# A causal attention stage on Trainium2: score tiles made once and kept, values as the moving side

## The reference

```python
x = layernorm(x + linear_attention(x))      # stage A, 16 heads, chunks of 64
x = layernorm(x + fp8_gated_ffn(x))         # stage B, hidden 2048
x = layernorm(x + causal_attention(x))      # stage C, one head of width 128
x = layernorm(x + base + low_rank_experts(x))  # stage D, 6 experts of rank 16, top 2
```

```python
q, k, v = x @ Wq + bq, x @ Wk + bk, x @ Wv + bv
scores = q @ k.T / sqrt(128)                # causal mask: -inf above the diagonal
out = softmax(scores) @ v @ Wo + bo
```

## Time and profile before

| | |
|---|---|
| time, three runs | 1518.12, 1520.05, 1521.35 us; median 1520.05 |
| the profiled execution's own time | 1522.29 us |
| its span, first to last instruction | 1520.5 us |
| granted TensorE clock, mean of the span | 0.989 |
| TensorE matmul busy | 1463.3 us, 96% |
| TensorE weight loads busy | 1004.2 us, 66% |
| VectorE busy | 1008.0 us, 66% |
| ScalarE busy | 734.4 us, 48% |
| GpSimd busy | 344.0 us, 23% |

### The profile page before, as it was taken

How to read it: one execution, slowest core, us unless ns; L and a number is a source line. 1 busy time by engine, 2 the same in 40 slices (tenths; PEclk the granted TensorE clock), 3 DMA queues, 4 the chain that set the end, 5 groups by cost and what they waited for, 6 DMA issues and landing times.

```text
span 1520.5 us, 23833 instructions
## 1 busy us (share of the span) xinstructions
PE 1463.3 (96%) x9472; PEld 1004.2 (66%) x9472; DVE 1008.0 (66%) x1966; ACT 734.4 (48%) x1039; POOL 344.0 (23%) x259
## 2 busy tenths in 40 slices
PE   8999999999999999899999999989999999999998
PEld 6677777777777776444554555546656666677886
DVE  3355555464646467888778778874888888566665
ACT  4333333333333335777877876853434444432333
POOL 0021211120211123000000000001657676750001
PEclk9999999999999999999999999999999999999999
DMA  7203031212130251001100100013100000000112
GB/s 269 81 27 109 28 110 33 104 55 89 49 108 1 87 188 42 14 1 56 56 28 28 56 29 27 1 42 114 37 1 1 1 0 1 0 1 28 56 56 83
DMA packets 43905, 79.93 MB, mean 53 GB/s; under 512 B 7074, under 2 KB 14882, under 8 KB 42387
## 3 DMA queue, kind: packets, MB, share of 16 engines
q1 hardware_dynamic: 43794, 78.41, 15.3%
HBM read 53.24 MB, written 25.17 MB: 52 GB/s over the span
## 4 chain that ended last, share of the span: by engine, by line
PE 63%; issue 19%; DVE 13%; ACT 3%; POOL 1%; DMA 0%; SPq 0%; DVEq 0%; POOLq 0%; ACTq 0%
PE psum L125 13%; PE psum L127 12%; PE psum L126 12%; PE psum L1360 6%; PE psum L1003 3%; PE psum L1010 3%; PE psum L616 2%; DVE sm L464 2%; PE psum L1338 2%; PE psum L642 2%; PE psum L631 2%; PE psum L637 2%; DVE c_mx L1281 1%; PE psum L651 1%; PE psum L646 1%
## 5 line engine op out<-in xcount | busy, mean ns | idle before, releaser
L1003 PE MATMUL psum<-early,high 128*128 128x512 fp8e4 x1024 | 235.0, 382 | 7.9 <-DVE low_r L975 4.2
L1003 PEld LDWEIGHTS psum<-early,high 128*128 128x128 fp8e4 x1024 | 98.2, 98 | 127.7 <-ACT early L880 6.6
L1209 POOL TENSOR_TENSOR c_ls<-c_ls,c_pr 128x512 f32<-128x512 f32 (+2 forms) x136 | 161.9, 1190 | 65.5 <-ACT c_pr L1254 56.3
L410 POOL TENSOR_TENSOR rms<-ms,mhalf 128x16 f32<-128x16 f32 x30 | 87.8, 2926 | 341.9 <-DVE ms L473 341.9
L1254 ACT ACTIVATE c_pr<-c_sc 128x512 f32<-128x512 f32 (+2 forms) x144 | 85.1, 593 | 152.7 <-DVE c_sc L1296 137.7
L1360 PE MATMUL psum<-c_pr,V 128*128 128x512 f32 (+2 forms) x288 | 138.1, 565 | 3.7 <-ACT c_pr L1254 2.5
L125 PE MATMUL psum<-Qh_r,Kh 128*128 128x512 f32 (+1 forms) x272 | 139.7, 513 | 0.0
L1010 PE MATMUL psum<-high,b_act 128*128 128x512 fp8e4 x512 | 118.9, 387 | 2.4 <-DVE Ql_r L980 2.2
L1296 DVE TENSOR_TENSOR c_sc<-psum,c_mb 128x512 f32<-128x512 f32 (+2 forms) x144 | 91.8, 640 | 42.8 <-PE psum L127 32.7
L125 PE MATMUL psum<-early_r,high_r 128*128 128x512 f32 x256 | 106.6, 417 | 5.4 <-DVE early_r L436 5.4
L127 PE MATMUL psum<-Qh_r,Kl 128*128 128x512 f32 (+1 forms) x272 | 105.2, 387 | 0.0
(11 more groups left out here) (238 smaller groups left out, 3245.8 us busy)
## 6 DMA issues: line engine op xcount, KB each, us to landing
low<-x_dram SPq DMA_DIRECT2D x9, 1024.0 KB, 5.5
wst<-in_L_ffn_w_gating SPq DMA_DIRECT2D x16, 512.0 KB, 4.5
xs<-in_L_attn_x SPq DMA_DIRECT2D x8, 1024.0 KB, 7.3
xt<-in_x_turned SPq DMA_DIRECT2D x7, 1024.0 KB, 5.0
x_dram<-xs SPq DMA_DIRECT2D x7, 1024.0 KB, 4.8
x_dram<-low SPq DMA_DIRECT2D x5, 1024.0 KB, 4.3
wst<-in_L_ffn_w_linear SPq DMA_DIRECT2D x16, 256.0 KB, 4.5
high<-x_dram SPq DMA_DIRECT2D x4, 1024.0 KB, 6.6
```

The costliest lines, as they stand in the source:

```text
L410: nc.gpsimd.tensor_tensor(rms_of(b, c), ms_of(b, c), const["mhalf"][:, 0:H], ALU.pow).then_inc(*done)
L1003: last = t.matmul(out[:, h, :], w8g[:, tile + k, (2 * m + h) * P:(2 * m + h + 1) * P], x8[:, u, k, :], start=k == 0, stop=k == DC - 1)
L1209: nc.gpsimd.tensor_tensor(ls[:, i % 2, q0:], ls[:, i % 2, q0:], pr[:, g % SLOTS, q0:], ALU.add).then_inc(*L.done(*name))
```

## The change

The scores of a tile are made once (`r`, three matmuls and the mask, keys as rows). ScalarE, for every fourth tile VectorE, copies them to a place on chip; VectorE takes the maximum with a running tile `gm` of 128 x 512, element by element. When a whole block is there, `gT` transposes `gm` (4 transposes), one reduction gives `nm` for all four chunks, and `dm`, `mb` follow as before. Then GpSimd adds `mb` in place, two tiles at a time (five pairs of the last block on VectorE), ScalarE takes the exponential in place over both, and `pv` multiplies: the exponentials are now the stationary side, 128 queries by 128 keys, and the values with a column of ones, 129 wide, the moving side. The ones give the row sums, so `ls`, `sum` and `L` go. The totals of all blocks after the first lie in banks 5 and 6; `on` copies them, `oT` transposes them (4 transposes), and `oh`, `ol`, `y` follow as before.

The places (`homes`) are pairs of tiles: 5 of their own, 6 in `Qh` and `Ql` where the queries are no longer wanted, and 8 in `xs` of blocks 0 to 3, which are stored to DRAM after their `norm` and loaded again for stage D (`spill`). Stage D therefore takes the blocks in the order 4, 5, 6, 0, 1, 2, 3, 7, and its weights are split into `Qh` and `Ql` when their last tiles are used. `order` says when scores are made by a table (`points`) of how many should be there at how many used, if a home is open. Stage C's first jobs now stand among stage B's last ones.

The diff, cut to its core:

```diff
+    homes = [("rows", n) for n in range(OWN)] + [(w, b) for b in (0, 2, 4) for w in ("Qh", "Ql")] + [("x3", n) for n in range(2 * SPILL)]
...
+    def home_of(home):
+        w, n = home
+        if w == "rows":
+            return rows[:, 2 * n - 2:2 * n, :] if n else first_rows[:, :, :]
+        if w == "x3":
+            return high[:, n // 2, 2 * (n % 2):2 * (n % 2) + 2, :]
+        return (Qh32 if w == "Qh" else Ql32)[:, n:n + 2, :]
...
+    raws = [("r", i, k) for i in range(NB) for k in range(tiles(i))]
+    points = [(4, 16), (9, 24)] + [(2 * (i + 1) * (i + 2) - 8, 2 * (i + 2) * (i + 3)) for i in range(2, NB - 1)] + [(10 ** 6, len(raws))]
...
+    def open_home():
+        for home in sorted(unused, key=lambda h: (h[0] not in ("Qh", "Ql"), last_use.get(h, (0, 0))[0])):
+            w, n = home
+            _, i, k = raws[made]
+            if i >= NB - 2 and k >= 2 * NB and w in ("Qh", "Ql"):
+                continue
+            if home in last_use or w == "rows" or (w == "x3" and n // 2 in ended and sum(x[0] == "pv" for x in order[ended[n // 2]:]) >= 6) or (w in ("Qh", "Ql") and made >= 2 * (n + 2) * (n + 3)):
+                return home
+        return None
+    def emit_raw():
+        nonlocal made
...
+    def emit_pv(i, k, n):
+        order.append(("pv", i, k))
+        if k % 2 or n == 2:
+            home = place[i, k // 2]
+            unused.append(home)
+            last_use[home] = (len(order), ("pv", i, k))
...
+    emit_raws(4)
+    order += [("gT", 0), ("bias", 0), ("mb", 0)]
+    for k in range(CH):
+        if k % 2 == 0:
+            emit_raws(2)
+        emit_pv(0, k, 1)
+    emit_raws(6)
+    order.append(("gT", 1))
+    emit_raws(2)
+    order.append(("mb", 1))
+    consumed, since = CH, 0
+    for i in range(1, NB):
+        outputs = [("oT", i - 1)] + [("y", i - 1, c) for c in range(CH)]
+        for u, (k, n) in enumerate(units(i)):
+            while made < len(raws) and made < wanted(consumed + n) and emit_raw():
+                pass
+            whole_block = i + 1 < NB and made >= 2 * (i + 2) * (i + 3)
+            if whole_block and since >= 2 and ("gT", i + 1) not in order:
+                order.append(("gT", i + 1))
+                since = 0
+            elif whole_block and since >= 2 and ("mb", i + 1) not in order:
                 order.append(("mb", i + 1))
-            order.append(("pv", i, k))
-            if tail and (k == 1 or k >= 3):
-                order.append(tail.pop(0))
-        order += tail
-    order += [("L", NB - 1)] + [("y", NB - 1, c) for c in range(CH)]
+            emit_pv(i, k, n)
+            consumed += n
+            since = since + n if whole_block else 0
+            if outputs and (u != 1 or i == 1):
+                order.append(outputs.pop(0))
+                if not outputs:
+                    ended[i - 1] = len(order)
+        order += outputs
...
+        if i + 1 < NB:
+            while made < 2 * (i + 2) * (i + 3):
+                assert emit_raw()
+            order += [x for x in (("gT", i + 1), ("mb", i + 1)) if x not in order]
+            since = 0
+    order += [("oT", NB - 1)] + [("y", NB - 1, c) for c in range(CH)]
+    on_dve = {x[1:] for n, x in enumerate(raws) if n % 4 == 3}
...
+    subs_on_dve = {(NB - 1, k) for k in range(2, CH * (NB - 1), 6)}
+    def soften(i, k):
+        while to_sub and to_sub[0] <= (i, k + 9):
+            x = to_sub.pop(0)
+            (dve_order if x in subs_on_dve else pool_order).append(("sub", *x))
+        while to_exp and to_exp[0] <= (i, k + 5):
+            act_order.append(("exp", *to_exp.pop(0)))
...
+        if kind == "r":
+            (dve_order if name[1:] in on_dve else act_order).append(("cp", *name[1:]))
+            dve_order.append(("max", *name[1:]))
+            if name[1:] == (1, CH):
+                pool_order.append(("bo", NB - 1))
+        elif kind == "gT":
+            dve_order.append(("nm", i))
+            act_order += [("dm", i, q) for q in range(CH)]
+            if i:
+                pool_order.append(("bo", i - 1))
...
+        elif kind == "mb":
+            act_order.append(("mb", i))
+            to_sub += [(i, k) for k, _ in units(i)]
+            to_exp += [(i, k) for k, _ in units(i)]
+            soften(i, -3)
+        elif kind == "pv":
+            soften(i, name[2])
+            if name[2] == tiles(i) - 1:
+                act_order.append(("on", i))
+                dve_order.append(("rl", i))
+        elif kind == "oT":
...
+            w, n_r = (4, 5)[n_r % 2] if n_r < 4 else n_r % (2 if i < 2 else 3), n_r + 1
...
+        banks[name] = (w,) if kind != "pv" else (5, 6) if i else (2, 3)
...
+    def totals(i):
+        w = 5 if i else 2
+        return psum[:, w:w + 2, 0:2 * VN].rearrange("p b (u n) -> p b u n", u=2)
...
+    def spill(sp):
+        for b in range(SPILL):
+            wait_for(sp, 0, (A, ("norm", b, CH - 1)))
+            sp.dma_start(x3_dram[b], xs[b]).then_inc(spilled[b], 16)
+        for b in range(SPILL):
+            sp.wait_ge(spilled[b], 16)
+            for half in range(2):
+                if ("x3", 2 * b + half) in last_use:
+                    wait_for(sp, 0, (M, last_use["x3", 2 * b + half][1]))
+            sp.dma_start(xs[b], x3_dram[b]).then_inc(back_in[b], 16)
...
+                wait_for(pool, 0, (A, ("mb", i)), copied(i, k), copied(i, k + (k < CH * i)))
+                if k < CH * i:
+                    both = home_of(place[i, k // 2])
+                    nc.gpsimd.tensor_tensor(both, both, mb[i % 2][:, None, :].broadcast_to([P, 2, BT]), ALU.add).then_inc(*L.done(*name))
                 else:
-                    wait_for(pool, 0, (L, ("sum", i, k - 1)))
-                    nc.gpsimd.tensor_tensor(ls[:, i % 2, q0:], ls[:, i % 2, q0:], pr[:, g % SLOTS, q0:], ALU.add).then_inc(*L.done(*name))
+                    q0 = (k - CH * i) * P
+                    row = row_of(i, k)[:, q0:]
+                    nc.gpsimd.tensor_tensor(row, row, mb[i % 2][:, q0:], ALU.add).then_inc(*L.done(*name))
...
+            if kind == "cp":
+                k = name[2]
+                q0 = max(0, k - CH * i) * P
+                copy_needs(act, i, k)
+                nc.scalar.activation(row_of(i, k)[:, q0:], bank_of("r", i, k)[:, q0:], ACT.Identity).then_inc(*A.done(*name))
+            elif kind == "on":
+                wait_for(act, 0, (M, ("pv", i, tiles(i) - 1)), *([(M, ("oT", i - 1))] if i else []))
+                nc.scalar.activation(on[:, :, :].rearrange("p (b u) n -> p b u n", u=2), totals(i)[:, :, :, 0:P], ACT.Identity).then_inc(*A.done(*name))
...
+            else:
+                k = name[2]
+                wait_for(act, 0, less_max(i, k))
+                if k < CH * i:
+                    both = home_of(place[i, k // 2])
+                    nc.scalar.activation(both, both, ACT.Exp, scale=scale).then_inc(*A.done(*name))
+                else:
+                    row = row_of(i, k)[:, (k - CH * i) * P:]
+                    nc.scalar.activation(row, row, ACT.Exp, scale=scale).then_inc(*A.done(*name))
...
+            elif kind == "max":
+                k = name[2]
...
+                if (i, k) not in on_dve:
+                    needs.append((A, ("cp", i, k)))
+                wait_for(dve, 0, *needs)
+                if k == 0:
+                    nc.vector.tensor_copy(out, row).then_inc(*done)
+                else:
+                    nc.vector.tensor_tensor(out, row, out, ALU.max).then_inc(*done)
...
-                nc.vector.reciprocal(rl[:, :], bank_of("L", i)[:, 0:CH]).then_inc(*done)
+                wait_for(dve, 0, (M, ("pv", i, tiles(i) - 1)), (A, ("on", i)), *([(V, ("y", i - 1, CH - 1))] if i else []))
+                nc.vector.reciprocal(rl[:, :].rearrange("p (b u) -> p b u", u=2), totals(i)[:, :, :, P]).then_inc(*done)
...
+            elif kind == "r":
...
+            elif kind == "gT":
+                wait_for(pe, 0, *needs, (V, ("max", i, tiles(i) - 1)))
+                for c in range(CH):
+                    last = nc.tensor.transpose(out[:, c * P:(c + 1) * P], gm[:, i % 2, c * P:(c + 1) * P], ident[:, :])
+            elif kind == "mb":
+                wait_for(pe, 0, *needs, (A, ("dm", i, CH - 1)))
+                last = nc.tensor.matmul(out[:, :], oner, dm, start=True, stop=True, skip_group_check=True)
             elif kind == "pv":
                 k = name[2]
-                g = sum(tiles(j) for j in range(i)) + k
-                q0 = max(0, k - CH * i) * P
-                keys = slice(k * P, (k + 1) * P)
+                n = 2 if k < CH * i else 1
                 wait_for(pe, 0, *needs, (A, ("exp", i, k)))
-                last = nc.tensor.matmul(out[:, q0:], values[:, keys], pr[:, g % SLOTS, q0:], start=k == 0, stop=k == tiles(i) - 1, skip_group_check=True)
-            elif kind == "L":
-                wait_for(pe, 0, *needs, (L, ("sum", i, tiles(i) - 1)))
+                for tile in range(k, k + n):
+                    row = row_of(i, tile)
```

(33 more changed lines are left out.)

305 lines of the change are left out of this document (150 added, 155 removed).

## The result

The changed kernel took 1557.19 us (median of four runs, 1555.43 to 1558.38) against 1520.11 us before: ratio 1.024, 95% interval 1.0223 to 1.0257. It is slower by 37 us, and I had forecast 18 us faster.

A forecast was written before the change was run, and what follows sets the result against it. Stage C was taken to be bound by TensorE with a tenth of slack. Work -28.2, pauses +(41 - 29), stage B's filled gaps -2 gave -18 us from a median of 1520.05: 1502 us, range 1493 to 1512.

The forecast's parts named there:

- What TensorE saves: TensorE's work in stage C: maxima, `L` and old values products removed, new values products and transposes added, -28.2 us.
- rival (c): New values products: weight loads don't hide beneath matmuls, 1056 x 0.11 us more, 1615 us; chance 0.03.
- the sum of the pauses: Stage C: TensorE's pauses, 41 us against 29 before; under 30 or over 55 would show the prediction wrong.
- The copy `on` and `rl` that free banks 5 and 6 (0.9 us) lie inside these.: Block boundaries: freeing the totals' banks adds nothing to the exposed pauses, which sum to 26.3 us.
- queued behind exponentials that wait for GpSimd: Block starts: ScalarE's copies wait, and TensorE waits for the banks, 0.5 to 1 us a block, 4 in all.
- The serial chain: Block boundaries: `gT` to `mb` 3.0 us and `mb` to first `pv` 4.7, partly covered; 26.3 us exposed in all.
- Stage D's roundings: Block 7: weight roundings moved there, 5 x 0.6 us on ScalarE and 5 x 0.69 on VectorE, cost nothing.
- if stage B or D changes by more than 5: Stages B and D: a change of more than 5 us in either would show the prediction wrong.
- The clock: Block boundaries: granted clock falls to 0.50 after pauses, at most one counted per boundary, 4 x 1.8 = 7 us.
- (a): Block boundaries cost little and the clock holds: pauses 15 to 25 us, 1476 to 1486 us; chance 0.24.
- (b): GpSimd's pair additions set the pace if over 3.2 us each; at 4.0 the time is 1543 us; chance 0.10.
- (d): VectorE takes over in units with a `y`, needing 4.5 us; gain cancelled, no change, 1520 us; chance 0.05.

The follow-up runs named there:

- run 1: The changed kernel with the totals' copy `on` ahead of the next block's first exponentials in ScalarE's order: 1541.14 us.
- run 5: The changed kernel with `on` ahead of the next block's first exponentials and exponentials queued 3 tiles ahead of their product instead of 5: 1537.77 us.
- run 12: The last kernel of Runs 9 to 11 with all eight score copies of block 1 on VectorE, which did two before: 1516.04 us.
- run 7: Run 5's kernel with `nb` as a product on GpSimd, and the last block's five pair additions also on GpSimd instead of VectorE: 1532.28 us.
- Runs 9 to 11: Added in turn to run 7: `bo` behind its block's last addition, 1526.19 us; `nm` ahead of queued statistics, 1525.06; blocks 1 to 7's first pair tile by tile, 1519.24.
- after: The changed kernel as first made, against the kernel before at 1520.11 us: 1557.19 us, ratio 1.024.
- runs 6 and 7: The first is run 5's kernel with `nb` as a product on GpSimd and means negated on VectorE: 1533.62 us; the second is run 7.
- run 4: The changed kernel with extra unread products in blocks 1 to 7, eight between `gT` and `mb`, ten ahead of the first `pv`: 1560.99 us.
- Run 3: The changed kernel without the addition of the negated maxima, the exponential's scale a hundredth as large; part of the computation is left out: 1509.7 us.
- run 13: Run 12's kernel with stage D's five weight roundings on VectorE behind the rounded parts of its first four x tiles: 1513.93 us.
- run 8: Run 5's kernel with the first pair addition of blocks 1 to 7 on VectorE instead of GpSimd: 1543.95 us.

## Why the prediction was wrong

**What TensorE saves: right.** Forecast -28.2 us, measured about -26. The passes step by 0.111 us with their weight loads beneath (rival (c) falls). The pair addition (2.4) and the pair exponential (1.05) cost what they were priced at. The rule of the Trainium skill that I had weighed there (page "TensorE: Matmul & The Clock Gate", Part 3, "The mechanism": a load overlaps matmuls in flight only in another row group) would make the step 0.22 us, by the forecast's estimate; the trace does not agree, with 0.111. A sentence earlier in the same section also lets a load run ahead that goes to a background weight buffer; the trace does not speak against that one.

**The failed step** is the sum of the pauses, forecast as 41 us against 29 before. In the account above, over a wider stretch, pauses and rest are 110 us against 48: 62 us more where I had 12. By the forecast's own measure, the 336.8 us from first to last `pv` less the 242 of work that its sums leave are some 95 us, far over the 55 that it had named as a sign of being wrong. The first part of the step is the sentence "The copy `on` and `rl` that free banks 5 and 6 (0.9 us) lie inside these." They don't lie inside; they stand behind. I priced the copy's own length and not its place in ScalarE's in-order queue, behind two exponentials that are each held by a 2.35 us addition, themselves behind a `bo` of 4.57, and at block 4 behind two normalizations too. The three boundaries where `rl` ends the pause took 17.8 us, and were priced at 9.6; moving `on` alone gave back 16 us (run 1). The second part is the sentence on ScalarE's copies "queued behind exponentials that wait for GpSimd", at "0.5 to 1 us a block, 4 in all". The mechanism was right and the size was not: TensorE's pauses ended by `max` are 21.1 us, against 7.4 before by the old maxima and 7 priced in all (4 here, 3 for the banks of blocks 0 and 1), and the edits that take copies out from behind exponentials gave back 22 us together (19 in run 5, with `on`, and 3 in run 12).

**The serial chain: right in size where it stood alone.** 15.7 us priced, 16.4 measured, for the first three boundaries. I had missed `bo` in it, 2 us at block 2 in run 7, and the statistics ahead of `nm`. Runs 9 to 11 together gave 13 us for the order and the first piece of the chain.

**Stage D's roundings: wrong.** "5 x 0.69 on VectorE", with the result "nothing", counted engine time over a whole block. In after one of them took 2.83 us, in run 12 two took 5.40 beside GpSimd's additions; they stood ahead of the x tiles that stage D's first product needs, and made a pause of 4.4 to 5.1 us (2.1 and 2.9 in runs 6 and 7). The bound that I had set, "if stage B or D changes by more than 5", did not find it, since that pause lies ahead of the last `pv`; the stretch behind is 163.7 us in both.

**The clock: too small.** Seven us were put for it. The rest grew by 19, and I put most of that down to half clock: the mean clock of the stretch fell from 0.98 to 0.90. It goes with the pauses: run 4 raised the clock and was not faster, though it can't price the clock by itself.

**Rivals.** (a) fell with the pauses. (b) came nearest: GpSimd does set the pace, though not by its rate. At 2.4 us an addition it has room inside a block; it is at the starts of blocks, and through another engine's queue, that it holds TensorE. Run 3 bounds what hangs on its additions: 47 us. I had written in (b) "ScalarE's copies wait in order behind its exponentials" as a point in its favour, and then judged it by the rate alone. (d) did not show.

**Still open.** Of TensorE's 26 us of saved work, run 13 turns 6 into time. Its pauses (37.4) are still above those of before (23.9): the two chains before `mb` of blocks 2 and 3 (2.19 and 2.99 us), and score products that wait for `max` (10.3 us). Whether a different use of the homes, with the next block's scores made earlier, would cover them wasn't tried. Nor was splitting `bo`.

## What to carry to other kernels

For each wait, price not the instruction that ends it but everything that stands ahead of it in its engine's queue, and what that waits for in turn. An instruction that only frees a buffer is on the critical path when the next user stands ready; put it ahead of work that waits for a slower engine. Work that waits should not be queued earlier than it is needed: here less lead for the exponentials gave 12 us. At a serial boundary, cut the first piece small: the first tile alone gave 6 us here, by which TensorE started 2.7 us earlier at one block and then found its next work ready.

## What the runs showed of the hardware

In these traces an operation of VectorE with both inputs in SBUF that starts beside a GpSimd addition is held until that addition ends. `nb`, four elements a partition, starts at 1177.07 during `bo` and ends at 1180.83; `bo` ends at 1180.80. All six `nb` of after that meet an addition end within 0.03 us of its end. An addition of VectorE at 1369.13, beside only GpSimd's small `rstd`, took 1.22 us, and the shortest one is 1.21. At its shortest `nb` takes 0.15 us, in the kernel before its mean is 0.63, after the change 1.97. In run 12 roundings took 5.40 us for two of 128x512 and 2.88 for one of 113x512 beside additions, where the same operation with one input in PSUM (L1797) takes 0.69. It works the other way too: in run 8 a GpSimd addition that starts during VectorE's takes 3.33 instead of 2.35 us. The Trainium skill, page "SBUF — State Buffer", section "Who interferes with whom", says that a VectorE instruction with two SBUF inputs contends with a GpSimd instruction that reads SBUF, for a port pair that is held exclusively. The trace agrees, with the 0.03 us between the two ends. When something waits behind, it counts: the pause that run 13 took away was 5 us.
